# Two routings whose table of places is made batch by batch, with the place as a scalar of each partition

## The chip, the cores and the metric

The kernel runs on 1 core of one Trainium2 chip. The metric is the device time of one execution in microseconds. Three executions of the kernel before gave 327.29, 327.85 and 329.17 us; their median is 327.85 us. One more execution was profiled, and all rows below come from that one: it took 328.26 us, of which the profile's span covers 326.5 us.

## The reference

The input is x, 16 batches of 128 tokens with 128 features (2048 tokens in all), and a context of the same size. Four residual blocks follow each other:

```python
x = x + tanh(g_xattn[0]) * L0_xattn(layernorm(x), ctx, ctx, ...)   # autocorrelation, one weight per delay
x = x + tanh(g_ffn[0])   * L0_ffn(layernorm(x), ...)               # 8 experts, top 1, SiLU gate
x = x + tanh(g_xattn[1]) * L1_xattn(layernorm(x), ctx, ...)        # softmax attention, 16 heads of 8
x = x + tanh(g_ffn[1])   * L1_ffn(layernorm(x), ...)               # 8 experts, 2 per token, ReLU
```

In L0_ffn a token goes to the expert with the largest routing probability; in L1_ffn to the experts h and h+1 modulo 8, where h is an integer made from the first two features of the normalised token. Neither block needs an expert's product for a token that is not sent there.

## The kernel before, in words

The tokens lie as 128 partitions (token within the batch) by 16 batches. The program has four stages, A to D, one for each block. Every engine has its own list of steps, written out by hand in program order (lists PE, DV, AC, SP, PO); the engines meet only at semaphores. No scheduler moves anything. TensorE is kept busy between its steps by products without use, `warm(eng, bank, n)` (line 334), whose counts stand in the tuple `WARM`.

Stages B and D are the expert blocks. Ahead of each, `route` (lines 720 to 824) sorts the 2048 tokens by their expert, so that each tile of 128 sorted slots needs only the experts that occur in it. It does so in these steps:

- `rank_pe` (line 697) counts on TensorE how many tokens stand before each one, into `bank[3]`. VectorE turns that into each token's slot, less 63.5 (lines 737 and 739), and splits the slot into the start of its tile (line 740) and the place within the tile, 0 to 127 (line 742).
- Two tables are then made. `ohk` [128, 16, 3, 16] says for each token and each of the 16 tiles whether its slot lies there (line 741); ScalarE and VectorE multiply that by the token's number in its batch (line 797) and by the batch's number (line 744). `ohp` [128, 16, 128], in bf16, is the table of places: for each token and each place 0 to 127 it holds 1 where they are equal (line 747). Before the change two operations make it, one for eight batches each; both operands are broadcast views (`bc`): the row of numbers `iota_pb` is repeated over the batches, and each place in `place_b` over 128 columns.
- TensorE adds up 16 products, one per batch, of `ohp[:, b, :]` and the two parts of `ohk` (line 807). Its sum says for each place and tile which token stands there. It waits for semaphore `hot` before batch 0 and again before batch 8.
- VectorE reads the sum (lines 751 and 752) and makes the list of indices `inv_i`, by which GpSimd gathers the rows of the sorted tokens with indirect DMAs (`gather`, lines 1126 and 1363). Further small operations of VectorE (lines 755 to 776) make the list of jobs, that is, which tile meets which expert; TensorE needs it for its products at line 812 and, through registers, for all jobs but the first.

Between the table and line 751 VectorE has the step `beside`: in the first routing this is `gate_sums` (lines 942 to 944), two operations; in the second it is empty. `ohp` is read once more, in stage B alone, at line 1010.

The jobs of stage B (23) and of stage D (39) then run one after the other: up products (lines 993 and 1219) and down products (lines 1001 and 1229) on TensorE, with VectorE and ScalarE between them. Nothing in the program waits for a fixed time; each stage starts from what the one before it has made.

In the rows TensorE's bank 4 carries the name `pairA`, of whose memory it is a part, and `r16` the name `r`.

Of the kernel before, what the change touches and what calls it, by code (L numbers as in the profile page):

```python
# [37 lines left out]
def build(nc, A, out):  # L38
    f32, bf16, i32 = mybir.dt.float32, mybir.dt.bfloat16, mybir.dt.int32
    ALU, ACT, AX = mybir.AluOpType, mybir.ActivationFunctionType, mybir.AxisListType.X  # L40
    ds = bass.ds

    NB, T, D = A["x"].shape
# [20 lines left out]
    MIDDLE = (T - 1) / 2  # L64
    PARTS = 3
    SK = PARTS * PARTS * HD
    SM = SK + PARTS
    ROWS = 5
    ONES = 1.0019378662109375
    HU = H // 2  # L70
    NU = 2 * NB
# [10 lines left out]
    def sb(name, shape, dt=f32):  # L82
        return ctx.enter_context(nc.sbuf_tensor(name, shape, dt))

    def sem(name):
        return ctx.enter_context(nc.semaphore(name))

    def bc(ap, at, n):

        shape = list(ap.shape)  # L90
        return ap.unsqueeze(at).broadcast_to(shape[:at] + [n] + shape[at:])
# [4 lines left out]
    with ctx:  # L96
# [24 lines left out]
        iota_e = sb("iota_e", [128, NE])  # L121
        iota_p = sb("iota_p", [128, T])
        iota_pb = sb("iota_pb", [128, T], bf16)
        place_b = sb("place_b", [128, NB], bf16)
        part = sb("part", [128, 1])
        edge = sb("edge", [128, 2])
        jobs_to = sb("jobs_to", [128, 2, 2])
# [66 lines left out]
        r16 = sb("r16", [128, 8, NB])  # L194
        total = sb("total", [128, NE])
        maxp = sb("maxp", [128, NB])
        ohp = sb("ohp", [128, NB, T], bf16)
# [30 lines left out]
        def s(name):  # L228
            if name not in S:
                S[name] = sem("s_" + name)  # L230
            return S[name]
# [488 lines left out]
        def route(nth, jobs, fills, beside, behind):  # L720
# [5 lines left out]
            earlier = nth - 1  # L726
# [5 lines left out]
            def dve(eng):  # L732
# [2 lines left out]

                rank = bank[3][:, 0:NB * NE].rearrange("p (b e) -> p b e", e=NE)
                c.link(eng.scalar_tensor_tensor(lw[:, 2, :, :], rank, -MIDDLE, oh[:, :, :], ALU.add, ALU.mult))
                slot, start = (r16[:, k, :] for k in (0, 7))
                c.link(eng.reduce_sum(slot, lw[:, 2, :, :], AX))
                c.link(eng.tensor_scalar(start, slot, T * ROUND, -T * ROUND, ALU.add, ALU.add))  # L740
                eng.tensor_tensor(ohk[:, :, 0, :], bc(tile_at[:, :], 1, NB), bc(start, 2, TT), ALU.is_equal).then_inc(s("tile"), 1)
                eng.scalar_tensor_tensor(place_b[:, :], slot, MIDDLE, start, ALU.add, ALU.subtract).then_inc(s("tile"), 1)
                eng.wait_ge(s("tile"), 2 * earlier + 1)
                eng.tensor_tensor(ohk[:, :, 2, :], ohk[:, :, 0, :], bc(iota_pb[:, 0:NB], 2, TT), ALU.mult).then_inc(s("hotb"), 1)
                eng.wait_ge(s("tile"), 2 * earlier + 2)
                for half in (slice(0, NB // 2), slice(NB // 2, NB)):
                    eng.tensor_tensor(ohp[:, half, :], bc(iota_pb[:, :], 1, NB // 2), bc(place_b[:, half], 2, T), ALU.is_equal).then_inc(s("hot"), 1)
                beside(eng, c)

                eng.wait_ge(s("inv"), nth)  # L750
# [49 lines left out]
            def pe2(eng):  # L800
                warm(eng, bank[5], ranked)
                eng.wait_ge(s("hotk"), nth)
                eng.wait_ge(s("hotb"), nth)
                for b in range(NB):
                    if b % (NB // 2) == 0:
                        eng.wait_ge(s("hot"), 2 * earlier + 1 + b // (NB // 2))
                    i = eng.matmul(bank[4][:, 0:2 * TT].rearrange("p (a k) -> p a k", a=2), ohp[:, b, :], ohk[:, b, 1:3, :],
                                   start=(b == 0), stop=(b == NB - 1))
                i.then_inc(s("inv"), 1)
                warm(eng, bank[5], placed)  # L810
                eng.wait_ge(s("job_made"), 3 * earlier + 1)
                eng.matmul(at_tile, part[0:TT, :], begun[:, 2, 0:jobs], start=True, stop=True)
                eng.matmul(at_back, back, begun[:, 2, 0:jobs], start=True, stop=True).then_inc(s("job_sums"), 1)
                warm(eng, bank[5], cast)
            PE.append(pe2)

            def seg_pe(eng):
# [1144 lines left out]
```

## Time and profile before

| | |
|---|---|
| median of 3 runs | 327.85 us (327.29 to 329.17) |
| the profiled execution | 328.26 us |
| its span | 326.5 us |
| TensorE busy | 296.4 us |
| VectorE busy | 194.2 us |
| ScalarE busy | 165.0 us |
| GpSimd busy | 133.4 us |
| mean granted TensorE clock | 0.992 of full speed |

The difference of 1.76 us between the execution and its span lies outside what the profile sees. Starts are counted from the beginning of the span. Busy shares are averages over all stages: a stage in which TensorE waits for VectorE has to be read in the chain of waits and in the order of time.

### The profile page before, as it was taken

How to read it: one execution, taken by the hardware profiler on the slowest of the kernel's cores; microseconds unless marked ns; L12 is line 12 of the kernel's file. 1: busy time of each engine (PE TensorE's matmuls, PEld its weight loads, DVE VectorE, ACT ScalarE, POOL GpSimd, SP SyncE). 2: the span in 40 equal slices, each digit the busy share in tenths (PEclk: the TensorE clock that was granted, in tenths of full speed). 3: DMA queues.
4: the chain of work that ended last, by engine and by line, in shares of the span. 5: the costliest groups of instructions: out<-in, count | busy, mean ns of one | idle time of the engine just before them, and what ended most of it. 6: DMA issues, size and time to landing. Idle time of an engine off the chain costs nothing.

```text
span 326.5 us, 8565 instructions
## 1 busy us (share of the span) xinstructions
PE 296.4 (91%) x2896; PEld 242.9 (74%) x2908; DVE 194.2 (59%) x598; ACT 165.0 (51%) x344; POOL 133.4 (41%) x316
## 2 busy tenths in 40 slices
PE   8897998898999999986899999989779999999995
PEld 3546774697998999643577877767346999999995
DVE  7638769353434333374678888873686565556663
ACT  1253341543544553440676668778403665556561
POOL 7742311732364333134565546461114245552232
PEclk9999899999999999999999999999999999999999
DMA  7919978277121000517666565306982111111000
GB/s 198 372 61 331 359 223 266 67 154 155 49 64 42 24 26 24 145 33 202 143 148 166 144 151 125 70 5 190 292 294 67 50 42 50 51 50 33 18 19 24
DMA packets 34977, 40.22 MB, mean 123 GB/s; under 512 B 4556, under 2 KB 30191, under 8 KB 33775
## 3 DMA queue, kind: packets, MB, share of 16 engines
q1 hardware_dynamic: 29064, 31.81, 34.0%
q0 software_dynamic: 2560, 6.30, 6.6%
q10 hardware_dynamic: 3312, 1.58, 1.7%
q8 instruction: 25, 0.41, 0.5%
q14 instruction: 16, 0.13, 0.2%
HBM read 28.87 MB, written 10.50 MB: 121 GB/s over the span
## 4 chain that ended last, share of the span: by engine, by line
PE 69%; DVE 14%; DMA 6%; issue 4%; ACT 3%; POOL 2%; SPq 0%; DVEq 0%; ACTq 0%; POOLq 0%
PE bank L1229 11%; PE pairA L993 6%; PE pairA L1219 6%; PE pairB L1219 5%; PE bank L1001 5%; PE pairB L993 5%; PE bank L1741 4%; PE pairA L1711 4%; DMA qs<-rows_b_d,inv_i 3%; PE pairB L1727 3%; DVE maxi L1811 2%; PE pairB L334 2%; DMA x<-in_x 2%; PE pairB L611 1%; DMA qs<-qparts_d 1%
## 5 line engine op out<-in xcount | busy, mean ns | idle before, releaser
L1811 DVE TENSOR_REDUCE maxi<-pairA 128x8 f32<-128x1024 f32 x30 | 36.6, 1220 | 14.2 <-PE pairA L1711 14.1
L1229 PE MATMUL bank<-wring,prob 128*128 (+1 forms) x312 | 42.0, 277 | 0.1
L1229 PEld LDWEIGHTS bank<-wring,prob 128*128 128x128 f32 x312 | 38.2, 192 | 1.6 <-issue 1.2
L1783 ACT ACTIVATE prob<-pairB 128x1024 f32<-128x1024 f32 x30 | 30.7, 1023 | 14.5 <-PE pairB L1727 14.5
L1370 POOL DMA_INDIRECT out_x<-qs,inv_i x16 | 15.7, 980 | 34.0 <-DVE qs L1324 34.0
L1127 POOL DMA_INDIRECT qs<-rows_b_d,inv_i x16 | 15.6, 972 | 33.1 <-DVE big L1076 18.8
L1051 ACT ACTIVATE xn<-wring 128x1024 f32 x22 | 23.1, 1051 | 8.5 <-issue 7.7
L1279 ACT ACTIVATE xn<-wring 128x516 f32 x37 | 23.5, 635 | 7.6 <-issue 7.2
L290 POOL TENSOR_TENSOR lnv<-lnv,neg_half 128x4 f32<-128x4 f32 (+1 forms) x12 | 14.8, 1230 | 30.8 <-DVE lnv L285 30.8
L1001 PE MATMUL bank<-wring,prob 128*128 x184 | 24.7, 277 | 1.4 <-DVE prob L1081 1.4
L1364 POOL DMA_INDIRECT qs<-rows_d_d,inv_i x16 | 15.5, 967 | 24.4 <-DVE big L1317 12.8
L1132 POOL DMA_INDIRECT back_d<-qs,inv_i x16 | 15.6, 975 | 22.2 <-DVE qs L1101 22.2
L334 PE MATMUL pairB<-fill_b,onesb 128*128 128x512 bf16 x95 | 23.0, 396 | 1.7 <-POOL fill_b L380 1.5
L1001 PEld LDWEIGHTS bank<-wring,prob 128*128 128x128 f32 x184 | 22.3, 192 | 2.1 <-issue 1.8
L993 PE MATMUL pairB<-big,xn 128*128 x176 | 21.8, 277 | 1.4 <-DVE big L1076 1.2
L1741 PE MATMUL bank<-prob,vpad 128*32 128x128 f32 x512 | 20.6, 278 | 2.6 <-ACT osb L1779 2.0
L993 PEld LDWEIGHTS pairB<-big,xn 128*128 128x128 f32 x176 | 20.5, 192 | 1.9 <-issue 1.8
L993 PE MATMUL pairA<-big,xn 128*128 x176 | 21.4, 275 | 0.0
L303 ACT ACTIVATE xn<-x,lnv 128x128 f32<-128x128 f32 x36 | 15.7, 481 | 11.2 <-POOL lnv L292 11.2
L1293 ACT ACTIVATE prob<-pairB,xn 128x128 f32<-128x128 f32 x36 | 11.2, 363 | 19.1 <-PE pairB L1219 19.1
L1324 DVE SCALAR_TENSOR_TENSOR qs<-bank,job,qs 128x128 f32 x39 | 13.6, 349 | 11.8 <-PE bank L1229 11.8
L993 PEld LDWEIGHTS pairA<-big,xn 128*128 128x128 f32 x176 | 20.5, 192 | 0.0
(311 smaller groups left out, 645.7 us busy)
## 6 DMA issues: line engine op xcount, KB each, us to landing
wring<-in_wts SPq DMA_DIRECT2D x8, 768.0 KB, 7.9
wring<-in_wts SPq DMA_DIRECT2D x8, 514.0 KB, 5.0
ks<-kparts_d SPq DMA_DIRECT2D x12, 192.0 KB
qs<-qparts_d SPq DMA_DIRECT2D x12, 192.0 KB
kparts_d<-parts SPq DMA_DIRECT2D x8, 192.0 KB
qparts_d<-parts SPq DMA_DIRECT2D x8, 192.0 KB, 2.5
ctx_s<-kparts_d SPq DMA_DIRECT2D x6, 192.0 KB
ctxT<-qparts_d SPq DMA_DIRECT2D x6, 192.0 KB
```

The source lines that it names most:

```text
L303: return eng.activation(xn[:, b, :], x[:, b, :], ACT.Identity, bias=NMR[:, b:b + 1], scale=RSTD[:, b:b + 1])
L334: eng.matmul(bank_, onesb[:, :], fill_b[:, :], start=True, stop=True)
L993: j = eng.matmul(P[:, g_, o * T:(o + 1) * T], w[:, f * 128:(f + 1) * 128], tile_of(xT_all, tau, 0), start=True, stop=True)
L1001: j = eng.matmul(bank[1 + i % 2][:, 0:D], act[:, i % 2, c_, :], tile_of(wring, e, 2 * F0 + c_ * D), start=(c_ == 0), stop=(c_ == C0 - 1))
L1051: eng.activation(ups[:, i % 2, :], wring[:, ds(e, 1), 0:2 * F0].rearrange("p a w -> p (a w)"), ACT.Copy).then_inc(n["ups"], 1)
L1219: j = eng.matmul(P[:, g_, o * T:(o + 1) * T], w[:, f * 128:(f + 1) * 128], tile_of(xT_all, tau, 0), start=True, stop=True)
L1229: j = eng.matmul(bank[1 + i % 2][:, 0:D], act[:, i % 2, c_, :], down_weights(e, o), start=(c_ == 0), stop=(c_ == C1 - 1))
L1279: eng.activation(ups[:, i % UP, :], wd[:, ds(e, 1), 0:F1 + C1].rearrange("p a w -> p (a w)"), ACT.Copy).then_inc(n["ups"], 1)
L1370: eng.indirect_dma_start(out=out.rearrange("b t d -> (b t) d"), out_offset=bass.IndirectOffsetOnAxis(ap=inv_i[:, t:t + 1], axis=0), in_=xs ...
L1741: i = eng.matmul(bank[1][32 * p:32 * p + 32, u * T:(u + 1) * T], v[:, 32 * odd:32 * odd + 32], prob[:, at.half(6), 2 * p + odd, :], start= ...
L1783: eng.activation(prob[:, at.half(5), :, :].rearrange("p h t -> p (h t)"), turned_in(at.unit(5))[:, :, :].rearrange("p a t -> p (a t)"), AC ...
L1811: eng.reduce_max(maxi[:, at.half(0), :], scores_in(at.unit(0))[:, :, :].rearrange("p a (h t) -> p (a h) t", t=T), AX).then_inc(s("mx"), 1)
```

## The change

One instruction per batch takes the place of one per eight batches. Each compares the plain row `iota_pb` of 128 numbers, in bf16, with one value in each partition, the place of that partition's token in batch b. That value is now kept in f32, in a part of `r16` that was not in use, and the tile `place_b` is gone. The semaphore `hot` is still raised twice in each routing, after batch 9 and after batch 15 instead of after batches 7 and 15, and TensorE waits for it before batch 0 and before batch 10. The order of all other work stays as it was; three more lines make the numbers of later lines differ by 2 or 3.

```diff
--- before.py
+++ after.py
@@ -66,6 +66,7 @@
     SK = PARTS * PARTS * HD
     SM = SK + PARTS
     ROWS = 5
+    HOT = ((0, 10), (10, NB))
     ONES = 1.0019378662109375
     HU = H // 2
     NU = 2 * NB
@@ -121,7 +122,6 @@
         iota_e = sb("iota_e", [128, NE])
         iota_p = sb("iota_p", [128, T])
         iota_pb = sb("iota_pb", [128, T], bf16)
-        place_b = sb("place_b", [128, NB], bf16)
         part = sb("part", [128, 1])
         edge = sb("edge", [128, 2])
         jobs_to = sb("jobs_to", [128, 2, 2])
@@ -735,16 +735,18 @@
 
                 rank = bank[3][:, 0:NB * NE].rearrange("p (b e) -> p b e", e=NE)
                 c.link(eng.scalar_tensor_tensor(lw[:, 2, :, :], rank, -MIDDLE, oh[:, :, :], ALU.add, ALU.mult))
-                slot, start = (r16[:, k, :] for k in (0, 7))
+                slot, place, start = (r16[:, k, :] for k in (0, 6, 7))
                 c.link(eng.reduce_sum(slot, lw[:, 2, :, :], AX))
                 c.link(eng.tensor_scalar(start, slot, T * ROUND, -T * ROUND, ALU.add, ALU.add))
                 eng.tensor_tensor(ohk[:, :, 0, :], bc(tile_at[:, :], 1, NB), bc(start, 2, TT), ALU.is_equal).then_inc(s("tile"), 1)
-                eng.scalar_tensor_tensor(place_b[:, :], slot, MIDDLE, start, ALU.add, ALU.subtract).then_inc(s("tile"), 1)
+                eng.scalar_tensor_tensor(place, slot, MIDDLE, start, ALU.add, ALU.subtract).then_inc(s("tile"), 1)
                 eng.wait_ge(s("tile"), 2 * earlier + 1)
                 eng.tensor_tensor(ohk[:, :, 2, :], ohk[:, :, 0, :], bc(iota_pb[:, 0:NB], 2, TT), ALU.mult).then_inc(s("hotb"), 1)
                 eng.wait_ge(s("tile"), 2 * earlier + 2)
-                for half in (slice(0, NB // 2), slice(NB // 2, NB)):
-                    eng.tensor_tensor(ohp[:, half, :], bc(iota_pb[:, :], 1, NB // 2), bc(place_b[:, half], 2, T), ALU.is_equal).then_inc(s("hot"), 1)
+                for lo, hi in HOT:
+                    for b in range(lo, hi):
+                        i = eng.tensor_scalar(ohp[:, b, :], iota_pb[:, :], place[:, b:b + 1], None, ALU.is_equal)
+                    i.then_inc(s("hot"), 1)
                 beside(eng, c)
 
                 eng.wait_ge(s("inv"), nth)
@@ -802,8 +804,9 @@
                 eng.wait_ge(s("hotk"), nth)
                 eng.wait_ge(s("hotb"), nth)
                 for b in range(NB):
-                    if b % (NB // 2) == 0:
-                        eng.wait_ge(s("hot"), 2 * earlier + 1 + b // (NB // 2))
+                    for n, (lo, _) in enumerate(HOT):
+                        if b == lo:
+                            eng.wait_ge(s("hot"), 2 * earlier + 1 + n)
                     i = eng.matmul(bank[4][:, 0:2 * TT].rearrange("p (a k) -> p a k", a=2), ohp[:, b, :], ohk[:, b, 1:3, :],
                                    start=(b == 0), stop=(b == NB - 1))
                 i.then_inc(s("inv"), 1)
```

The order on VectorE in the first routing, before the change. In these rows `s_hot`, `s_tile`, `s_chain_dve`, `s_lexp`, `s_inv` are semaphores, and x2 means two alike in a row.

```order
L741 TENSOR_TENSOR ohk<-tile_at,r 128x16x16 [waits s_chain_dve]
L742 SCALAR_TENSOR_TENSOR place_b<-r 128x16
L744 TENSOR_TENSOR ohk<-ohk,iota_pb 128x16x16 [waits s_tile]
L747 TENSOR_TENSOR ohp<-iota_pb,place_b 128x1024 [waits s_tile]
L747 TENSOR_TENSOR ohp<-iota_pb,place_b 128x1024
L943 TENSOR_REDUCE r<-lw 128x16 [waits s_lexp]
L944 RECIPROCAL r<-r 128x16 [waits s_chain_dve]
L751 COPY inv<-pairA 128x16 [waits s_inv,s_chain_dve]
```

The same place on VectorE after the change:

```order
L741 TENSOR_TENSOR ohk<-tile_at,r 128x16x16 [waits s_chain_dve]
L742 SCALAR_TENSOR_TENSOR r<-r 128x16
L744 TENSOR_TENSOR ohk<-ohk,iota_pb 128x16x16 [waits s_tile]
L748 TENSOR_SCALAR ohp<-iota_pb,r 128x128 [waits s_tile]
L748 TENSOR_SCALAR ohp<-iota_pb,r 128x128 x15
L946 TENSOR_REDUCE r<-lw 128x16 [waits s_lexp]
L947 RECIPROCAL r<-r 128x16 [waits s_chain_dve]
L753 COPY inv<-pairA 128x16 [waits s_inv,s_chain_dve]
```

Sixteen short instructions of another kind stand where two long ones stood, and nothing else has changed its place. In the second routing the two rows after them are missing, before and after alike.

The order on TensorE at the same place, before the change (the x13 and x12 at line 334 are products without use):

```order
L334 MATMUL pairA<-fill_b,onesb 128x512 x13
L807 MATMUL pairA<-ohk,ohp 128x32 [waits s_hot,s_hotb,s_hotk]
L807 MATMUL pairA<-ohk,ohp 128x32 x7
L807 MATMUL pairA<-ohk,ohp 128x32 [waits s_hot]
L807 MATMUL pairA<-ohk,ohp 128x32 x7
L334 MATMUL pairA<-fill_b,onesb 128x512 x12
```

And after the change:

```order
L334 MATMUL pairA<-fill_b,onesb 128x512 x13
L810 MATMUL pairA<-ohk,ohp 128x32 [waits s_hot,s_hotb,s_hotk]
L810 MATMUL pairA<-ohk,ohp 128x32 x9
L810 MATMUL pairA<-ohk,ohp 128x32 [waits s_hot]
L810 MATMUL pairA<-ohk,ohp 128x32 x5
L334 MATMUL pairA<-fill_b,onesb 128x512 x12
```

The second wait has moved from the ninth product to the eleventh. The same holds for the second routing.

## Rows read from the trace of the kernel before

**Rows 1.** The page: TensorE's share, and the chain that ended last by engine.

```profile
PE 296.4 (91%) x2896; PEld 242.9 (74%) x2908; DVE 194.2 (59%) x598; ACT 165.0 (51%) x344; POOL 133.4 (41%) x316
...
PE 69%; DVE 14%; DMA 6%; issue 4%; ACT 3%; POOL 2%; SPq 0%; DVEq 0%; ACTq 0%; POOLq 0%
```

**Rows 2.** Chain of waits, 48 to 72 us: start us, us, what.

```profile
52.38 2.27 DVE ohp L747 x2
54.65 0.21 DVE r L943
...
55.18 0.18 DVE inv L751
```

**Rows 3.** Chain of waits, 234 to 251 us.

```profile
240.35 2.28 DVE ohp L747 x2
...
242.68 0.37 PE pairA L807 x8
```

**Rows 4.** Order of time, first routing: start, duration, engine, line, [idle before, releaser].

```profile
52.30 2.35 DVE L747 TENSOR_TENSOR ohp<-iota_pb,place_b 128x1024 bf16<-128x1024 bf16 x2
...
53.66 0.35 PE L807 MATMUL pairA<-ohk,ohp 128*128 128x32 bf16 x8 [0.33 <-DVE ohp L747]
...
54.56 0.28 DVE L943 TENSOR_REDUCE r<-lw 128x16 f32<-128x128 f32 x1
...
54.70 0.37 PE L807 MATMUL pairA<-ohk,ohp 128*128 128x32 bf16 x8 [0.69 <-DVE ohp L747]
...
55.18 0.17 DVE L751 COPY inv<-pairA 128x16 f32<-128x16 f32 x1
...
55.48 0.23 DVE L948 TENSOR_SCALAR maxp<-r,tg 128x16 f32<-128x16 f32 x1
55.61 0.16 DVE L755 COPY total<-bank 128x8 f32<-128x8 f32 x1
...
55.86 1.23 POOL L1127 DMA_INDIRECT qs<-rows_b_d,inv_i  x1 [12.78 <-DVE inv_i L752]
```

**Rows 5.** Order of time, second routing.

```profile
240.27 2.35 DVE L747 TENSOR_TENSOR ohp<-iota_pb,place_b 128x1024 bf16<-128x1024 bf16 x2
...
242.68 0.37 PE L807 MATMUL pairA<-ohk,ohp 128*128 128x32 bf16 x8 [0.69 <-DVE ohp L747]
...
243.08 0.17 DVE L751 COPY inv<-pairA 128x16 f32<-128x16 f32 x1 [0.46 <-PE pairA L807]
```

**Rows 6.** Order of time, VectorE, 249 to 252 us.

```profile
248.97 0.61 DVE L1311 TENSOR_SCALAR prob<-pairA,wring 128x128 f32<-128x128 f32 x2 [1.00 <-PE pairA L1219]
249.50 0.19 DVE L790 TENSOR_TENSOR job<-bank,iota_p 128x40 f32<-128x40 f32 x1
249.72 0.24 DVE L791 TENSOR_SCALAR job<-job,half_gate 128x40 f32<-128x40 f32 x1
249.88 0.18 DVE L792 TENSOR_SCALAR job<-job 128x40 f32<-128x40 f32 x1
250.09 0.20 DVE L793 TENSOR_TENSOR job<-job 128x40 f32<-128x40 f32 x1
```

**Rows 7.** Order of time, VectorE, 138 to 150 us.

```profile
139.54 0.60 DVE L300 TENSOR_SCALAR xn<-x,lnv 128x128 f32<-128x128 f32 x2 [0.44 <-POOL lnv L290]
140.06 0.16 DVE L279 TENSOR_TENSOR lnv<-st 128x4 f32<-128x4 f32 x1
...
140.41 0.17 DVE L282 TENSOR_SCALAR lnv<-lnv 128x4 f32<-128x4 f32 x1
140.48 0.16 DVE L283 TENSOR_SCALAR lnv<-lnv 128x4 f32<-128x4 f32 x1
```

**Rows 8.** Stretches: start:end, us, busy by engine, clock, DMA share, GB/s.

```profile
29.00:30.00 1.00, 0.00 (x0) 0.00 (x0) 0.90 (x2) 1.00 (x3) 0.00 (x0) 1.00 1.02 406
31.00:35.00 4.00, 4.00 (x24) 4.00 (x23) 2.17 (x6) 0.60 (x1) 0.00 (x0) 0.57 1.03 429
```

**Rows 9.** Order of time, TensorE, ahead of the second routing.

```profile
237.38 0.23 PE L701 MATMUL bank<-ohb,before 128*128 128x136 bf16 x1 [1.17 <-DVE ohb L1909]
```

## The prediction

> **What bounds the kernel now.** I read the page first. TensorE is busy for 91% of the span, and the chain that ended last lies on it for 69%, but 14% of that chain is VectorE's [rows 1]. So I looked at the two routings in the chain of waits, since a share over the whole span says nothing of them. In both, the two operations that make the table of places stand in the chain with their whole length: 2.27 us in the first and 2.28 us in the second [rows 2, 3]. No other engine covers them. TensorE has run out of work ahead of them: it idles 0.33 us before its first product of the table and 0.69 us before the ninth [rows 4]. What follows hangs on them too: the list of indices, GpSimd's first gather at 55.86 us, which sat idle for 12.78 us until VectorE's indices came [rows 4], the list of jobs, and the jobs. So a microsecond more or less in the table is a microsecond of the kernel, in each routing.
>
> How the chain goes on differs. In the first routing it stays on VectorE: L943 starts at 54.56, L944 follows, and L751 starts at 55.18, while TensorE's last products, from 54.70 for 0.37 us, end at 55.07, 0.11 us sooner [rows 2, 4]. In the second routing nothing stands between: VectorE idles 0.46 us for the products, which start at 242.68, take 0.37 us, and let L751 start at 243.08 [rows 3, 5]. So in the first the time from the start of the table to L943 counts, and in the second the time to the last product.
>
> **What is removed.** Per routing two operations of 1024 columns. They start at 52.30 and L943 behind them at 54.56: 2.26 us, 1.13 us each [rows 4]. In the second routing the place of the ninth product at 242.68 gives the same: 2.35 us from the table's start to its end, and 0.06 us to the product [rows 5]. Of such an operation little is fixed: an operation of 4 columns without a scalar from memory takes 0.07 us from its start to the next one's, 140.41 to 140.48 [rows 7]. So a column costs (1.13 - 0.07) / 1020 = 1.04 ns, and the columns make up 1.07 us of the 1.13.
>
> **What is added.** Sixteen operations of 128 columns with one scalar of each partition. What counts is s, the time from one's start to the next one's. The trace has no such operation on bf16, so I bound it.
>
> The fixed part first. L948 has one such scalar and 16 columns, and the operation after it starts 0.13 us later [rows 4]; L791 has 40 columns and holds up the next for 0.16 us [rows 6]. Less 1.04 ns for each column these leave 0.113 and 0.118 us; if their columns ran faster, up to 0.14. The pair at L1311, 128 columns each with one scalar, source in the accumulation banks, takes 249.50 - 248.97 = 0.53 us, or 0.265 each [rows 6]; less 0.133 for the columns 0.132 us. So the scalar roughly doubles what an operation costs beside its columns: 0.11 to 0.14 us against 0.07.
>
> Then the columns. At 1.04 ns each, 128 cost 0.133 us, and s would be 0.246 to 0.265 us. The nearest row of all, L300, 128 columns of f32 in and out of SBUF with two scalars, agrees at (140.06 - 139.54) / 2 = 0.26 us [rows 7]. Against that, an operation with one tensor seems to take its columns faster than one with two: at 40 columns L792 lasts 0.18 us and L793, with two tensors, 0.20 [rows 6], which is half of 40 times 1.04 ns. If the two scalars of L300 cost more than one, its columns also ran at about half. The table's columns have half the bytes of these. If the time goes down with the bytes once more, they cost 0.033 us, and s is 0.146 to 0.173. At half a column's time they cost 0.067, and s is 0.18 to 0.21. The lowest bound is a scalar that costs nothing: 0.07 + 0.033 = 0.103 us. Ends are thus 0.10 and 0.265 us. I take 0.16, the columns at a quarter: a choice, since no row has bf16 here, and the 0.02 us between L792 and L793 is all that speaks for faster columns.
>
> The Trainium skill has the rule on this in "VectorE: DVE Perf Modes", section "The perf-mode tier table (the rule you actually need)": an operation with one bf16 tensor in SBUF reaches four elements a cycle, and one with two tensors at most two. The old operation did not even reach two, by its 1.04 ns a column; for the new one no run here shows it yet. By that rule, and the fixed parts above, s would be 0.146 to 0.173 us.
>
> **The sum.** First routing: 16 x 0.16 = 2.56 us against 2.26, so L943 and all behind it come 0.30 us later. TensorE's last six products hide behind L943 and L944 even better than the eight did. Second routing: the last operation starts at 15 x 0.16 = 2.40 us and lasts about 0.25 (L791 with its 40 columns lasts 0.24 [rows 6]), so it ends at 2.65 against 2.35, and the products start 0.30 us later. There are six of them after the last wait instead of eight. Eight take 0.37 us in rows 5 and 0.35 when they are the first eight [rows 4]; one alone lasts 0.18 by my estimate (their spacing then is about 0.03), so 0.06 us is gained. The second routing costs 0.24 us. Together +0.54 us.
>
> The other edits cost nothing. The scaling at L742 writes f32 instead of bf16 at the same size and place. The other wait of TensorE moves: the first ten tables are there 9 x 0.16 + 0.25 = 1.69 us after the start, plus the 0.14 us that lay between table and product before (one old operation lasts 2.35 - 1.13 = 1.22 us, and the product starts 1.36 us after the first), so at 1.83 against 1.36. TensorE then idles 0.80 instead of 0.33 us before the first product, has its ten done 0.45 us later, and idles about 0.4 us before the eleventh instead of 0.69. Ten are done well before the last six arrive; nothing queues there. Behind VectorE's table only what is in its list waits, and that is in the sum. GpSimd is idle at both places [rows 4], and no DMA is issued or awaited in the table's stretch by VectorE. Transfers after it (gathers, key loads) start from semaphores that the delayed work raises, so they are all moved by the same amount, and none meets another that it did not meet before.
>
> The profiled execution took 328.26 us, 1.76 of them outside the span. With +0.54 it would take 328.8. It stands 0.41 us above the median of the three runs, 327.85, so my time for a median is 328.4 us. A change of 0.5% (1.64 us) is about what a measurement of this kernel can tell from none; my +0.54 is a third of that.
>
> **Rivals.**
>
> 1. Columns at full cost. If a one-tensor operation on bf16 takes its columns one by one, as L300's 0.26 us may mean, s is 0.26: 16 x 0.26 = 4.16 us, 1.90 us more in the first routing, and 1.84 in the second. The kernel would take 331.6 us, 1.1% slower. The place is the same table, the mechanism is the operation's rate, and it decides from s = 0.196 us on, where 2 x (16 x s - 2.26) - 0.06 passes 1.64. For it: L300 and L1311 both at 0.26. Against it: L792 under L793. At half a column's time, s = 0.20, it would be +1.8 us, 329.6 us, right at the limit.
>
> 2. The scalar costs nothing when such operations follow each other, because the next one's scalar is read while the columns of the last one run. Then s is about 0.105: 1.68 us instead of 2.26, -0.58 and -0.64, -1.2 us in all, 326.6 us. For it: VectorE's operations overlap by about 0.08 us anyway (two of 1.22 us in 2.35). Against it: the pairs at L1311 and L300, which do follow each other, show 0.26. In the same page, section "The TRN2 errata — SBUF-src ops pay a fixed extra latency per instruction", the Trainium skill's table has 58 cycles and the columns over four, which is an estimate of 0.094 us for each, and -1.6 us for both routings. The same section warns that many small tiles each pay that latency where one large tile pays it once; by it the change gives away part of what faster columns bring, and the trace agrees that something is paid by each, 0.07 us without a scalar.
>
> 3. TensorE's clock falls. Ahead of 31 us TensorE did nothing in the whole stretch 29 to 30, and at 31 to 35 us it was granted 0.57 of full speed, though the same stretch shows it busy throughout [rows 8]. If the longer idle time at the table did that in one routing, the loss would be that of those rows, 4 x 0.43 = 1.7 us, on top of 0.5: 330.1 us. Against it: an idle time of 1.17 us ahead of L701 ahead of the second routing did not bring the mean of the span below 0.992, of which the stretch of rows 8 alone takes 1.7 of some 2.6 us [rows 9], and my 0.80 is shorter.
>
> 4. The change doesn't do what it says: the sixteen operations are split or held up by each other's semaphores. Only the tenth and the sixteenth raise one and only the first waits, so I give this nothing of its own.
>
> **How the numbers follow.** My case, s between 0.14 and 0.18, time within 327.8 to 329.1: 0.66. Half a column's time, around 329.3: 0.10, of which a third is over the limit. Rival 1 in full: 0.10. Rival 2: 0.11, with nearly all of it less than 0.5% below. Rival 3: 0.03. Slower by over 0.5%: 0.10 + 0.03 + 0.03 = 0.16. Faster by over 0.5%: 0.04, from rival 2 at its cheapest end together with the scatter of a median. The rest, 0.80, is within 0.5%. The range reaches down to rival 2 and up past the half column: 326.9 to 330.0 us. It leaves out rival 1 and the ends of the others.
>
> **What would show it.** In the profile after, the sixteen operations are one group: its count is 32, and the stretch from the first's start to L946's start, divided by 16, is s: 0.16 by my case, 0.26 by rival 1, 0.105 by rival 2. L754 (L752 of before) should end 0.30 us later counted from L741 in the first routing, and 0.24 in the second. TensorE's idle time should be 0.8 us before the first product of L810 and 0.4 before the eleventh, with a granted clock of 1.00 in both routings. All stages between the routings should keep their lengths. I am wrong in the step on columns if s is outside 0.14 to 0.18, and in the step on what lies on the path if s is right and the routings are not longer by those amounts.

## The result, and the profile after

| | changed | before, timed beside it |
|---|---|---|
| median | 331.07 us (22 runs, 328.3 to 341.84) | 328.77 us (22 runs, 327.15 to 334.4) |
| ratio | 1.0074, 95% interval 1.005 to 1.0098 | |
| the profiled execution | 329.11 us, span 327.3 | 328.26 us, span 326.5 |
| mean granted TensorE clock in it | 0.988 | 0.992 |

The medians are of all runs; the ratios, here and below, leave out those executions of either kernel that fell into a slower state of the device. The kernel became slower by 0.74%, 2.4 us. I had forecast 0.54 us, at 328.4 us, and "within 0.5%"; 331.07 us lies above the range's end of 330.0. The operation itself did what I had said. The page of the changed kernel answers to [rows 1]:

```profile
PE 298.3 (91%) x2896; PEld 242.4 (74%) x2908; DVE 195.3 (60%) x626; ACT 165.1 (50%) x344; POOL 133.9 (41%) x316
...
PE 71%; DVE 11%; DMA 5%; issue 4%; ACT 4%; POOL 3%; SPq 0%; DVEq 0%; ACTq 0%; POOLq 0%
```

VectorE has 626 counted operations instead of 598, the 28 that were added. The order of time in the first routing answers to [rows 4]:

```profile
50.68 3.74 PE L334 MATMUL pairA<-fill_b,onesb 128*128 128x512 bf16 x10
...
51.31 2.69 DVE L748 TENSOR_SCALAR ohp<-iota_pb,r 128x128 bf16<-128x128 bf16 x16
...
54.26 0.56 PE L810 MATMUL pairA<-ohk,ohp 128*128 128x32 bf16 x16
...
54.92 0.17 DVE L753 COPY inv<-pairA 128x16 f32<-128x16 f32 x1 [0.45 <-PE pairA L810]
```

And in the second, to [rows 5]:

```profile
240.38 2.69 DVE L748 TENSOR_SCALAR ohp<-iota_pb,r 128x128 bf16<-128x128 bf16 x16
...
242.24 0.40 PE L810 MATMUL pairA<-ohk,ohp 128*128 128x32 bf16 x10 [0.82 <-DVE ohp L748]
...
243.12 0.32 PE L810 MATMUL pairA<-ohk,ohp 128*128 128x32 bf16 x6 [0.48 <-DVE ohp L748]
...
243.47 0.18 DVE L753 COPY inv<-pairA 128x16 f32<-128x16 f32 x1 [0.41 <-PE pairA L810]
```

Sixteen operations take 2.69 us, and the table's rows by tile say that one lasts 248 ns, so s is (2.69 - 0.248) / 15 = 0.163 us. In the second routing L753 starts 3.09 us after the table's start, against 2.81 in [rows 5]: 0.28 us later. TensorE idles 0.82 and 0.48 us, where I had 0.8 and 0.4.

The first routing of this execution is disturbed: its first product waits for no table, since the products without use ahead of it were still running. The stretch in which they ran, and one behind the first wait for gathered rows in stage B (stretches: start:end, us, busy by engine, clock, DMA share, GB/s), for the changed kernel:

```profile
46.00:54.00 8.00, 7.21 (x36) 3.21 (x37) 7.44 (x38) 0.82 (x2) 0.00 (x0) 0.57 1.06 288
80.00:85.00 5.00, 5.00 (x45) 4.87 (x45) 1.95 (x5) 1.66 (x2) 1.83 (x2) 1.00 0.19 49
```

and for the kernel before:

```profile
46.00:54.00 8.00, 6.46 (x55) 3.73 (x55) 7.03 (x25) 0.97 (x3) 0.00 (x0) 1.00 0.84 249
80.00:85.00 5.00, 5.00 (x45) 4.87 (x45) 1.94 (x5) 1.66 (x2) 1.82 (x2) 1.00 0.32 71
```

The granted clock was 0.57 in 46 to 54 us, so TensorE stood at its lower level, 1.2 GHz, for most of it. That began before the table, and in another profile of the unchanged kernel (below) the same stretch has 0.79. So the fall there does not belong to the change. Where the first routing is undisturbed (in the runs of the changed kernel below) the change costs 0.32 us: 3.20 us from the table's start to L753, against 2.88. The sum is 0.60 us. Some 1.8 us of the 2.4 have no place in my prediction.

### The profile page after: what moved, and what is told of

Its sections match the earlier page's. It is cut to its first block, busy times and chain, and to the rows that moved or that the text cites. A ratio compares the mean times of both kernels' runs of the same rounds, so it can differ in the third digit from the quotient of the medians.

```text
span 327.3 us, 8593 instructions
## 1 busy us (share of the span) xinstructions
PE 298.3 (91%) x2896; PEld 242.4 (74%) x2908; DVE 195.3 (60%) x626; ACT 165.1 (50%) x344; POOL 133.9 (41%) x316
## 4 chain that ended last, share of the span: by engine, by line
PE 71%; DVE 11%; DMA 5%; issue 4%; ACT 4%; POOL 3%; SPq 0%; DVEq 0%; ACTq 0%; POOLq 0%
PE bank L1232 11%; PE pairA L996 6%; PE pairA L1222 6%; PE pairB L1222 5%; PE bank L1004 5%; PE bank L1744 5%; PE pairB L334 5%; PE pairB L996 5%; PE pairA L1714 4%; DMA qs<-rows_b_d,inv_i 3%; PE pairB L1730 3%; PE pairA L334 2%; DVE maxi L1814 2%; DMA qs<-qparts_d 1%; PE bank L1762 1%
## 5 line engine op out<-in xcount | busy, mean ns | idle before, releaser
L1786 ACT ACTIVATE prob<-pairB 128x1024 f32<-128x1024 f32 x30 | 30.7, 1024 | 14.5 <-PE pairB L1730 14.5
L334 PE MATMUL pairB<-fill_b,onesb 128*128 128x512 bf16 x95 | 23.7, 405 | 1.7 <-POOL fill_b L380 1.5
L334 PE MATMUL pairA<-fill_b,onesb 128*128 128x512 bf16 x77 | 20.5, 416 | 0.3
```

Of the source, the lines that this page charges most:

```text
L334: eng.matmul(bank_, onesb[:, :], fill_b[:, :], start=True, stop=True)
L1786: eng.activation(prob[:, at.half(5), :, :].rearrange("p h t -> p (h t)"), turned_in(at.unit(5))[:, :, :].rearrange("p a t -> p (a t)"), AC ...
```

## The experiments

The first question was whether TensorE's clock takes the missing time (rival 3), the second whether the longer path does it by what it moves. The edits show changed lines and a line or two around them; `...` stands for lines left out. The ratio is always to the kernel before, timed beside the others in the same series of runs: e1 to e4, e5 to e8, e9 to e12 and e13 to e16 are four such series, with medians of the kernel before of 329.18, 327.70, 326.56 and 326.99 us.

**The same two kernels again, and TensorE's idle time.** `e1_before` is the kernel before, `e2_after` the changed one. `e3` gives the changed kernel more products without use ahead of the table, `e4` gives the kernel before fewer:

```diff
-    WARM = (26, 14, 16, 13, 30, 12, 3, 12, 4, 13, 6, 2, 18)
+    WARM = (26, 14, 16, 16, 30, 12, 3, 12, 4, 16, 6, 2, 18)   # e3, on the changed kernel
+    WARM = (26, 14, 16, 11, 30, 12, 3, 12, 4, 11, 6, 2, 18)   # e4, on the kernel before
```

> The kernel before, run beside the others for its granted clock in each execution. By theory A (the change's own work costs about 0.5 us and the other 1.9 us come from a TensorE clock that falls more often or longer, because TensorE waits longer at the table) its mean granted clock is about 0.99, some 0.006 above that of the changed kernel, and times plotted against the clock lie on one line with those of the changed kernel, 0.5 us lower. By theory B (the sixteen operations cost 2.4 us on the path in most executions, and the clock is scatter that both kernels share) its mean clock is that of the changed kernel, and at equal clock it is 2.4 us faster.

> The changed kernel again. Both theories: 1.005 to 1.010 of the kernel before. A: mean granted clock about 0.984 and below that of the kernel before. B: the same clock as the kernel before.

> The changed kernel with three more products without use (16 instead of 13) ahead of the table's first product, in both routings. They fill about 0.65 us of the 0.8 us in which TensorE now waits for the first ten parts of the table, and end before these are there. A: the clock falls no more often than before the change, so about 1.0015 of the kernel before (+0.5 us), clock about 0.99. B: no change against the changed kernel, 1.007.

> The kernel before with two products without use fewer (11 instead of 13) ahead of the table's first product, in both routings: TensorE waits about 0.43 us longer there, as in the changed kernel, and nothing that is needed moves. A: slower by 1 to 2 us (1.003 to 1.006), with a lower clock. B: as the kernel before, 1.000.

Measured: e1 327.75 us, 0.9978 (0.9938 to 1.0018); e2 330.45, 1.0035 (0.9993 to 1.0078); e3 331.43, 1.0074 (1.0038 to 1.0109); e4 327.6, 0.9982 (0.9942 to 1.0023). Filling the idle time brings nothing back (e3), and a longer idle time in the kernel before costs nothing (e4). So rival 3 at the place where I had put it is not the cause. The intervals of e2 and of the first measurement overlap, though e2's just includes 1.

But the profile of e2 shows where time goes. TensorE in stage B, from 74 us, in e2, the last bracket being its idle time and what ended it:

```profile
76.64 1.95 PE L996 MATMUL pairB<-big,xn 128*128 x16
81.26 0.30 PE L982 MATMUL bank<-ident,qs 128*128 128x128 f32 x1 [2.67 <-DMA qs<-rows_b_d,inv_i]
81.51 2.02 PE L1004 MATMUL bank<-wring,prob 128*128 x8
83.32 2.75 PE L996 MATMUL pairA<-big,xn 128*128 x16
```

and in the kernel before:

```profile
75.69 1.95 PE L993 MATMUL pairB<-big,xn 128*128 x16
79.03 0.30 PE L979 MATMUL bank<-ident,qs 128*128 128x128 f32 x1 [1.39 <-DMA qs<-rows_b_d,inv_i]
79.28 1.15 PE L1001 MATMUL bank<-wring,prob 128*128 x8
80.27 1.95 PE L993 MATMUL pairA<-big,xn 128*128 x16
```

TensorE waits for a gathered tile 2.67 instead of 1.39 us, and behind that wait the same eight products take 2.02 instead of 1.15 us and the next sixteen 2.75 instead of 1.95. The granted clock of 80 to 85 us is 0.66 in e2 and 1.00 in the kernel before:

```profile
80.00:85.00 5.00, 3.74 (x17) 3.64 (x18) 1.24 (x3) 0.17 (x1) 0.95 (x1) 0.66 0.40 89
```

The fall costs 0.87 us in the eight products and 0.80 us in the sixteen, 1.67 us together. In e1 that stretch has 1.00, and it is 46 to 54 us that has the fall which I told of:

```profile
46.00:54.00 8.00, 7.77 (x53) 4.69 (x53) 6.41 (x24) 1.42 (x3) 0.00 (x0) 0.79 0.79 233
```

**One routing alone, and the delay alone.** `e5` makes the table the new way in the first routing only, `e6` in the second only. `e7` keeps the old table and adds two short operations on a spare tile behind it, so that the list of indices comes later by some 0.2 us in each routing, where the change costs 0.3:

```diff
+    NEW = (1,)        # e5; (2,) in e6
...
+                    if half.start:        # e7
+                        i = eng.tensor_tensor(spare[:, 0, :], iota_pb[:, :], iota_pb[:, :], ALU.is_equal)
+                        i = eng.tensor_tensor(spare[:, 1, 0:T // 4], iota_pb[:, 0:T // 4], iota_pb[:, 0:T // 4], ALU.is_equal)
```

> The change in the first routing alone; the second makes its table by two operations as before. From the profiles so far the changed table delays the indices by 0.32 us in the first routing and 0.28 in the second. Theory C (the rest of the loss arises in stage B: TensorE waits longer for a gather at about 79 us, beside the loads of keys, and its clock falls behind that wait): nearly the whole loss, 1.005, clock 0.985. Theory D (only the path is longer, and the rest is scatter of the clock): +0.3 us, 1.001, clock as the kernel before, 0.989.

> The change in the second routing alone. Theory C: +0.3 us, 1.001, clock 0.989 as before, and TensorE's wait for the gather at 79 us about 1 us as in the kernel before. Theory D: +0.3 us as well; the two differ in the other kernel. If this one shows more than 1.003 and the other does not, both are wrong.

> The kernel before, its table made by two operations as before, with two short operations on a tile without use behind them, 0.30 us in all, ahead of the second signal to TensorE, in both routings. The path gets as much longer as by the change, with none of its operations. Theory C (what counts is when the work behind the table starts): time and clock of the changed kernel, 1.005. Theory D: +0.6 us, 1.002, clock 0.989. If it stays at 1.002 while the changed kernel is at 1.005, something in the sixteen operations themselves, not the delay, makes the rest.

Measured: e5 330.47 us, 1.0060 (1.0021 to 1.0099); e6 328.08, 0.9993 (0.9953 to 1.0032); e7 327.97, 1.0002 (0.9965 to 1.0038). The loss comes with the first routing as far as the intervals tell (those of e5 and e6 just touch), and the delay by itself, 0.22 us there, does not make it. What e5 has and e7 hasn't is the sixteen operations themselves, and more instructions on VectorE ahead of stage B: 14 more than the kernel before, against two in e7.

**The operation by itself.** `e8` puts groups of sixteen operations of 128 columns (and a few of 1024) at the head of VectorE's list in the changed kernel, on tiles that are spare or written anew later. Its time, 357.24 us in its one execution, is of no use; its rows are.

> The changed kernel with 148 more operations at the head of VectorE's list, on tiles that are written anew later: groups of sixteen of 128 columns each (and two groups of two of 1024 columns), to measure one kind of operation at a time. Start to start: bf16 with a scalar from memory 0.16 us (the change's own). Bf16 with an immediate 0.10 to 0.11 if a scalar from memory costs 0.05 to 0.06, 0.16 if it costs nothing. F32 to f32 with a scalar 0.19 if its columns run at half of 1.04 ns, 0.26 if at the whole. F32 with two scalars 0.26 as L300. Two bf16 tensors of 1024 columns without a broadcast: 0.6 us if such columns run at half, 1.13 if not; with one broadcast operand likewise.

VectorE in order of time, the start of the program:

```profile
3.40 3.97 DVE L449 TENSOR_SCALAR ohp<-bench_s,bench_p 128x128 bf16<-128x128 bf16 x16
7.40 1.73 DVE L452 TENSOR_SCALAR ohp<-bench_s 128x128 bf16<-128x128 bf16 x16
9.16 3.22 DVE L455 TENSOR_SCALAR ohp<-bench_f,bench_p 128x128 bf16<-128x128 f32 x16
12.42 3.22 DVE L458 TENSOR_SCALAR prob<-bench_f,bench_p 128x128 f32<-128x128 f32 x16
15.67 2.25 DVE L461 TENSOR_SCALAR prob<-bench_f 128x128 f32<-128x128 f32 x16
17.96 4.18 DVE L464 TENSOR_SCALAR prob<-bench_f,bench_p 128x128 f32<-128x128 f32 x16
22.18 2.25 DVE L467 TENSOR_TENSOR ohp<-bench_s,qs 128x128 bf16<-128x128 bf16 x16
24.47 1.30 DVE L471 TENSOR_TENSOR ohp<-qs 128x1024 bf16<-128x1024 bf16 x2
```

From start to start, a sixteenth each: f32 with a number in the instruction (15.67 to 17.96) 0.143 us, with a scalar of each partition (12.42 to 15.67) 0.203, with two such scalars (17.96 to 22.18) 0.264. So each scalar from memory costs 0.06 us. On bf16 with a number in the instruction (7.40 to 9.16) it is 0.110 us; 0.053 more for the scalar is the 0.163 of the routing. The first group reads 0.250 us (3.40 to 7.40) for the same operation; GpSimd was busy beside it until 7.3 us, and in the routings it is idle. That it is GpSimd that makes it longer wasn't isolated. Two bf16 tensors of 1024 columns, plain, take 0.65 us each (24.47, two in 1.30), against the 1.13 us of the old table [rows 4], whose second operand is one value repeated over 128 columns.

**Instructions without any delay.** VectorE's program reaches it in pieces over the DMA engines, a transfer for each, on a queue that the profile marks as one of instructions. The transfers of 74 to 78.5 us by queue (packets, MB, share of 16 engines), in the kernel before:

```profile
q1 hardware_dynamic: 128, 0.68, 68.4%
q0 software_dynamic: 60, 0.16, 15.0%
```

and in the changed kernel, where the queue of VectorE's program, q14, comes to them (that it is VectorE's shows in e13 below, where 128 instructions more on VectorE bring one piece more on it):

```profile
q1 hardware_dynamic: 124, 0.67, 66.2%
q0 software_dynamic: 60, 0.16, 15.1%
q14 instruction: 1, 0.01, 0.6%
```

Each piece is 8 KB. The trace has them at 79.8 and 80.4 us in the kernel before, behind the key loads of q1, at 76.7 and 79.5 us in the changed one and 77.7 and 81.7 us in e2. VectorE stops at the same place in stage B for gathered rows, and with 14 more instructions ahead the end of a piece falls before that stop instead of behind it, as I read it from the times of the fetches. To test this without any longer path, `e9` puts 14 settings of a spare value into an idle time of VectorE ahead of the first routing, `e10` 32 of them into the changed kernel, 16 at that place and 16 in an idle time of stage A:

```diff
+            for k in range(14):        # e9, on the kernel before
+                eng.memset(spare[:, k:k + 1], 0.0)
             eng.wait_ge(s("consts"), 1)
             chosen(1, 0, NB - GB)
```

> The kernel before with 14 tiny operations more on VectorE (one value of a tile without use each), put where it sits idle for 2.2 us ahead of the first routing: no wait in the chain changes, only VectorE's program is longer by as many instructions as the change adds to the first routing. Theory E (the rest of the loss comes from where VectorE's next instructions are fetched: the profiles show a fetch of 8 KB at about 76.6 us, amid the loads of keys, in the kernels with the changed first routing, and at about 79.8 us, behind them, in the others): 1.004 to 1.006, the fetch at about 77 us and TensorE's wait for the gather above 2 us. Theory G (the rest comes from the sixteen operations themselves): 1.000, and the fetch plays no part.

> The changed kernel with 32 such tiny operations, 16 in an idle time of 2.6 us in stage A and 16 ahead of the first routing. By theory E the fetch moves forward to about 61 to 64 us, ahead of the loads of keys, so only the longer path is left: 1.002, wait for the gather 1.0 to 1.5 us. By theory G as the changed kernel, 1.006.

> The changed kernel once more, on the same chip as the two above. Both theories: 1.004 to 1.008; E: a fetch at about 77 us and a wait for the gather near 2 us in its profile.

Measured: e9 328.73 us, 1.0054 (1.0018 to 1.0089); e10 328.13, 1.0069 (1.0035 to 1.0102); e11, the changed kernel once more, 330.46 in six runs, 1.0102 (1.0054 to 1.0149). In e9 the table is the old one and takes as long as before (2.88 and 2.81 us to the copy), and still the kernel is 0.5% slower. Its stage B shows what e2's shows. TensorE:

```profile
78.34 0.30 PE L982 MATMUL bank<-ident,qs 128*128 128x128 f32 x1 [2.06 <-DMA qs<-rows_b_d,inv_i]
78.58 1.15 PE L1004 MATMUL bank<-wring,prob 128*128 x8
79.57 3.37 PE L996 MATMUL pairA<-big,xn 128*128 x16
```

The wait is 2.06 us, and the sixteen products behind it take 3.37 us instead of 1.95, at a granted clock of 0.67 (80 to 85 us). e10 is a miss. I had expected its time near 1.002, since it moves the pieces again: they lie at 50.2, 55.7, 60.1, 80.2 and 118.4 us, and its profile has no fall at 80 us. Its time stayed at 1.0069. Its twelve runs fall in two groups, six of 326.4 to 327.4 us and six of 328.9 to 330.8, and the profiled one (327.37 us) is of the first; what the second group does, no profile shows.

**A table that is faster.** `e12` keeps two operations per routing but turns the table, so that the batch lies innermost and no operand repeats a value over the innermost columns; a full table of numbers for it is made at the start on GpSimd. TensorE then reads `ohp[:, :, b]`, every sixteenth value:

```diff
-                    eng.tensor_tensor(ohp[:, half, :], bc(iota_pb[:, :], 1, NB // 2), bc(place_b[:, half], 2, T), ALU.is_equal).then_inc(s("hot"), 1)
+                    eng.tensor_tensor(ohp[:, :, half], iota_tb[:, :, half], bc(place_b[:, half], 1, T), ALU.is_equal).then_inc(s("hot"), 1)
```

> The kernel before with the table laid out as [place, batch] instead of [batch, place], and the numbers 0 to 127 as a full table made once by GpSimd while it is idle. Both operands of the comparison, and its output, then run over neighbouring values inside, as in the two operations without a repeated value that took 0.65 us for 1024 columns in e8_operations, against 1.13 us. VectorE's program has no more instructions for it. If the operations reach that: 1.0 us saved in each routing, 0.994 in all. If the short runs of 8 values hinder it, or TensorE reads its weights more slowly at a stride of 16 values, nothing or a loss.

> The kernel with the table turned (place outermost, batch innermost, both halves by two tensor_tensor operations as in the kernel before), once more. Its profile showed 0.76 us less from table to inverse in each routing, 1.5 us in all, and its timed ratio was 1.0001. If the shorter path shows at last, 0.995 (0.992 to 0.998); if the time is given back behind it, by waits that do not shorten, 1.000 as before.

VectorE of e12 in order of time:

```profile
50.75 1.28 DVE L750 TENSOR_TENSOR ohp<-iota_tb,place_b 128x1024 bf16<-128x1024 bf16 x2
...
52.87 0.17 DVE L754 COPY inv<-pairA 128x16 f32<-128x16 f32 x1 [0.35 <-PE pairA L810]
```

Two operations take 1.28 us instead of 2.35, and the copy starts 2.12 us after the table instead of 2.88 (2.05 instead of 2.81 in the second routing). That is 1.5 us less in both together, and it isn't in the time: e12 327.12 us, 1.0001 (0.9972 to 1.003); e15, the same kernel on another chip, 327.86, 1.0023 (0.9992 to 1.0053). I had expected 0.994 of e12. In the second routing the profiles show where it is given back. GpSimd's first gather and TensorE's first use of its rows, in e12, whose table starts at 238.93 us:

```profile
241.65 1.09 POOL L1367 DMA_INDIRECT qs<-rows_d_d,inv_i  x1 [7.83 <-DVE inv_i L755]
...
245.56 0.33 PE L1211 MATMUL bank<-ident,qs 128*128 128x128 f32 x1 [0.64 <-DMA qs<-rows_d_d,inv_i]
```

and in the kernel before, whose table starts at 240.27 [rows 5]:

```profile
243.75 1.10 POOL L1364 DMA_INDIRECT qs<-rows_d_d,inv_i  x1 [8.53 <-DVE inv_i L752]
...
247.06 0.33 PE L1208 MATMUL bank<-ident,qs 128*128 128x128 f32 x1
```

The gather is issued 2.72 us after the table's start instead of 3.48, but its rows are used 6.63 us after it instead of 6.79: TensorE now waits 0.64 us for them (0.85 in e15). Where the 0.76 us of the first routing go stays open; there the first product of stage B does come earlier by as much. No version here beats the kernel before.

**A whole piece more.** If it is the place of the pieces that counts, then a whole piece more must cost nothing, and 14 + 114 = 128 instructions must cure the changed kernel of all but its longer path. `e13` adds 128 to the kernel before, `e14` adds 114 to the changed one, half of them in each of two idle times of VectorE; `e16` is the kernel before once more:

```diff
                 if g == 2:
                     weighted(1)
+                    for k in range(57):        # e14; 64 in e13
+                        eng.memset(spare[:, 64 + k:65 + k], 0.0)
...
+            for k in range(57):
+                eng.memset(spare[:, k:k + 1], 0.0)
             eng.wait_ge(s("consts"), 1)
```

> The kernel before with 128 tiny memsets on VectorE (a spare tile, one value each) put where it waits for other engines, ahead of the first routing: 64 in the idle time after the second part of the column sums, 64 ahead of the wait for the constants. 128 instructions are one whole piece of VectorE's program, so every later piece ends at the same instruction as in the kernel before. Theory E (what matters is where a piece of VectorE's program is fetched relative to the key loads): the fetch stays behind the key loads (near 79 us), no stretch at 1.2 GHz at 80 to 85 us, ratio 1.000 (0.997 to 1.003), although nine times as many instructions are added as in the run with 14, which measured 1.0054. Rival F (more instructions on VectorE cost by themselves, or any change of the program's length does): 1.005 or more.

> The changed kernel with 114 tiny memsets in the same two places (57 and 57), so that with the 14 instructions that the change adds in the first routing VectorE's program is one whole piece longer when it leaves that routing. Theory E: the fetch of stage B falls behind the key loads again (near 79 us instead of 76 to 77), the wait of the gather's transpose is back at 1.4 to 1.9 us, and what is left is the longer path of the two routings, 0.6 us: ratio 1.002 (0.999 to 1.005). Rival F (the added instructions, or a scatter between programs that has nothing to do with the fetch): 1.007 as for the changed kernel, or more.

> The kernel before, against itself in the same call: 1.000 (0.997 to 1.003). It shows how far two sets of runs of the same program lie apart here.

| | us | ratio, 95% interval |
|---|---|---|
| e13, before + 128 | 327.26 | 1.0006 (0.9979 to 1.0034) |
| e14, changed + 114 | 328.16 | 1.0019 (0.9989 to 1.0049) |
| e16, before | 327.63 | 1.0019 (0.9985 to 1.0053) |

128 instructions cost nothing where 14 cost 0.5%, and the changed kernel with 114 more is at 1.0019, which is the 0.6 us of its two routings, as expected. (The intervals of e9 and e13, from two chips, still share 1.0018 to 1.0034.) The pieces are back behind the key loads: the transfers of 74 to 78.5 us in e14,

```profile
q1 hardware_dynamic: 119, 0.68, 67.0%
q0 software_dynamic: 60, 0.16, 14.8%
```

and those of 78.5 to 82 us, with both pieces:

```profile
q0 software_dynamic: 117, 0.32, 38.0%
q1 hardware_dynamic: 205, 0.03, 8.2%
q8 instruction: 1, 0.02, 3.1%
q14 instruction: 2, 0.02, 1.7%
```

The order of time of e14, where the new table is still the slower one (3.20 us from 51.76 to 54.96) and the wait in stage B is short:

```profile
51.76 2.69 DVE L751 TENSOR_SCALAR ohp<-iota_pb,r 128x128 bf16<-128x128 bf16 x16
...
53.62 0.40 PE L813 MATMUL pairA<-ohk,ohp 128*128 128x32 bf16 x10 [0.82 <-DVE ohp L751]
54.50 0.32 PE L813 MATMUL pairA<-ohk,ohp 128*128 128x32 bf16 x6 [0.48 <-DVE ohp L751]
...
54.96 0.17 DVE L756 COPY inv<-pairA 128x16 f32<-128x16 f32 x1
...
78.40 0.30 PE L987 MATMUL bank<-ident,qs 128*128 128x128 f32 x1 [0.89 <-DMA qs<-rows_b_d,inv_i]
78.78 1.15 PE L1009 MATMUL bank<-wring,prob 128*128 x8
79.77 1.95 PE L1001 MATMUL pairA<-big,xn 128*128 x16
```

**All the profiles together.** Each kernel has one profile, and all of them but e8's can be sorted by when the first piece of stage B after 70 us is fetched, against the last transfer of the key loads on q1:

| the piece is fetched | profiles | wait for gathered rows near 80 us | granted clock, 80 to 85 us | stage B, first to last up product |
|---|---|---|---|---|
| with the last of them or up to 1.2 us later | before, e1, e4, e6, e7, e10, e12 to e16 | 0.9 to 1.9 us | 1.00 in all eleven | 67.7 to 69.0 us |
| 2.8 to 4.4 us before the last | e2, e3, e5, e9, e11 | 2.1 to 4.0 us | 0.66 to 0.72 | 69.9 to 72.1 us |
| 1.7 us before the last | the changed kernel | 1.65 us | 1.00 | 68.3 us |

The granted clock fell behind that wait in five of six profiles with the moved fetch, and in none of eleven without it. In the sixth, of the changed kernel itself, the fetch was moved least.

## Why the prediction was wrong

- **The cost of the new operation: right.** 0.163 us from start to start, forecast 0.16, from rows of f32 and one difference of 0.02 us; with so little behind the choice of a quarter for the columns, that it hit so closely is partly luck. Rivals 1 (0.26) and 2 (0.105) fall. The parts fit too: e8 has 0.053 us for the scalar from memory and 0.110 for the rest, where I had 0.04 to 0.07 for the scalar, and 0.07 + 0.033 for fixed part and columns. (Rival 1's limit, by its own formula, is s = 0.194 us, not 0.196; nothing hangs on it.)
- **What lies on the path: right.** +0.32 us in the first routing (forecast 0.30), +0.28 in the second (0.24).
- **Rival 3: wrong as a cause in the place where I put it.** Idle times of 0.82 and 0.48 us at the table had a granted clock of 1.00 behind them in e14, and neither e3 nor e4 moved the time with them. But the thing itself, a longer wait of TensorE and a fall of its clock behind it, came in stage B, at the price that I had named: 1.67 us in e2, against my 1.7. I had given it a chance of 0.03, and had looked for it at the table alone.
- **The step that failed: "Transfers after it (gathers, key loads) start from semaphores that the delayed work raises, so they are all moved by the same amount, and none meets another that it did not meet before", and with it "All stages between the routings should keep their lengths".** One kind of transfer starts from no semaphore of the program: the pieces of VectorE's program, whose fetches went with its count of instructions (e9, e13). I had counted the 14 added instructions as time alone. As program they shift each later piece by 14 instructions, and a fetch of stage B moved from behind the key loads to among them; how far the loss is shown to come of that stands below. The first up product of stage B and the last lie 68.1 us apart in the kernel before (59.7 to 127.7 us) and 70.7 us in e2 (60.6 to 131.3).

The ratios add up. 14 more instructions, from e9: 0.0054 x 327 = 1.8 us. Longer path: 0.6 us. Together 2.4 us, what was measured, 0.0074. e5 should have 1.8 + 0.32 = 2.1 us, a ratio of 1.0065, and has 1.0060; e6 has only 0.28 us and shows nothing; e14 should have 0.6 us, 1.0018, and has 1.0019.

What the timed runs show is this: 14 instructions more on VectorE ahead of stage B, which lengthen no path, cost 0.5% (e9); 128 of them cost nothing that can be measured (e13); and the changed kernel loses most of its loss with 114 more (e14). That it is the place of the fetched piece which decides is argued. For it speaks the table of profiles: where the fetch was moved, the first longer wait for gathered rows was 2.1 us and more in five of six, and the clock fell behind it. But the profile of the changed kernel itself shows 1.7 us and no fall there, with a span only 0.8 us longer, though its timed runs are the slower ones: an execution does not always pay. And e10, whose fetch of stage B is in the old place, is slow all the same. It has other pieces elsewhere, one at 118.4 us where before it was 141; whether that is its reason stays open. I didn't move a fetch alone, with the instructions in place, and no run shows how one transfer of 8 KB keeps a gathered tile away for that long.

How much of the 1.8 us is the clock's is open as well. Each timed run has its mean granted clock on record. Over the runs behind the ratios it is lower than that of the kernel before beside it by 0.0016 to 0.0041 in e2, e3, e5, e9 and e11, by 0.0031 on the mean; 0.0031 x 327 makes 1.0 us, an estimate. Among the others it lies between 0.0029 lower (e6) and 0.0027 higher (e4), and e6 lost no time, so this is a sign and no proof.

The kernel before against itself gave 0.0022 less in e1 and 0.0019 more in e16, so a single ratio here is good to about 0.3%, and the agreement of the sums above to less than that is luck in part. The medians of the kernel before moved by more, from 326.56 to 329.18 us between series, and e9, e10 and e11 stand against the lowest of them; e9's own 328.73 us is not above what the kernel before had elsewhere. For their ratios speaks e12, in the same series, at 1.0001.

## What to carry to other kernels

Count an edit's instructions on each engine as well as their time. Where the summed path explains only a part of a loss and the rest comes from stages that weren't edited, add to the kernel before as many instructions without use in an idle time, and then as many as fill a whole piece: that takes two runs and can tell the path from the place of the program. It isn't sure: e10, with 32 more, did not fit. Before an operation is split for a better rate, look at why the large one is slow; here it was one operand's innermost repeat, and turning the tile made the table 1.4 us shorter than splitting it did (1.28 against 2.69 us), though no time of the kernel came of it.

## What the runs showed of the hardware that I had not expected

- VectorE's program comes in transfers of 8 KB on a queue of its own, 128 instructions each by e13 and e14, and 14 instructions more went with a loss of 1.8 us in 327 (e9). The Trainium skill, "Runtime: NRT & Kernel Launch", section "Instruction fetch mechanics", calls the cost of crossing the end of a block "mostly hidden"; its blocks are of 16 KiB, VectorE's here of 8 KB. Each transfer took 0.3 to 1.1 us in the profiles of the two kernels, and between 66 and 90 us VectorE idles for at most 0.33 us with nothing seen that ends it, in the kernel before and in the changed one alike. So as to VectorE's own time the trace agrees; the kernel's time, by e9 against e13, depends on how many instructions stand ahead, and the place of a piece is the likely reason.
- A setting of one value on VectorE costs little: 64 take 1.20 us in e13, 0.02 us each, and 128 in idle times left the time at 1.0006.
- A value repeated over the innermost columns takes a bf16 comparison of two tensors from 0.65 (e8) to 1.13 us [rows 4] at 1024 columns. A repeat in the outer place (e12, two in 1.28 us) does not.
- A scalar of each partition from memory costs 0.05 to 0.06 us in each instruction of 128 columns (e8).
